# Half of w_up as block products, with down's two accumulators in one bank and part of the quantization on GpSimd

## The reference

```python
w_bot = einsum('bg,got->bot', y, weight * mask);  h = einsum('bnt,bot->bno', x, w_bot) + bias
# _bitlinear(x, w): x quantized per row with 127/max|x|, w quantized to {-1,0,1}/scale
gate = silu(_bitlinear(h, w_gate)); up = _bitlinear(h, w_up)        # 512 -> 2048 each
out  = x + _bitlinear(gate * up, w_down)                            # 2048 -> 512
```

## Time and profile before

| what | value |
|---|---|
| median of the runs | 441.2 us |
| the profiled execution | 440.59 us, span 438.8 us |
| granted TensorE clock | 0.999 |
| PE busy | 425.5 us, 97% of the span |
| DVE busy | 363.5 us, 83% |
| ACT busy | 336.8 us, 77% |
| POOL busy | 205.3 us, 47% |

### The profile page before, as it was taken

The page is one execution under the profiler, slowest core; times in us unless marked ns, Lnnn a source line. Parts: engine busy times, 40 slices in busy tenths (PEclk is TensorE's granted clock), DMA queues, the critical chain, the costliest instruction groups (busy, mean ns, idle before and its releaser), DMA issues.

```text
span 438.8 us, 7668 instructions
## 1 busy us (share of the span) xinstructions
PE 425.5 (97%) x2318; PEld 257.5 (59%) x2318; DVE 363.5 (83%) x611; ACT 336.8 (77%) x474; POOL 205.3 (47%) x221
## 2 busy tenths in 40 slices
PE   4899999999999999999999999999999999999997
PEld 0234688888744455556555565655566555556555
DVE  0327768898897988899999999899999999899992
ACT  1215988778867976888888888888888888888871
POOL 0006999999149995142432423344142333414132
PEclk9999999999999999999999999999999999999999
DMA  7999999995142337254453635535263553535375
GB/s 277 404 396 408 308 335 339 313 251 144 36 98 48 61 66 187 48 145 85 134 120 73 146 70 143 97 118 120 76 157 64 135 115 100 120 87 142 80 162 154
DMA packets 104458, 69.79 MB, mean 159 GB/s; under 512 B 87280, under 2 KB 87536, under 8 KB 102896
## 3 DMA queue, kind: packets, MB, share of 16 engines
q1 hardware_dynamic: 103712, 67.13, 56.9%
q10 hardware_dynamic: 720, 2.36, 1.5%
HBM read 40.11 MB, written 8.39 MB: 111 GB/s over the span
## 4 chain that ended last, share of the span: by engine, by line
PE 59%; DMA 14%; issue 11%; DVE 9%; ACT 5%; POOL 1%; DVEq 0%; ACTq 0%; SPq 0%; POOLq 0%
PE ps L1308 15%; DMA wc<-wc 12%; PE ps L1171 11%; PE ps L1236 10%; PE ps L1126 8%; PE ps L1206 8%; PE ps L1164 4%; ACT wc L640 3%; DVE wc L954 3%; DVE wc L988 2%; DMA wc<-wcond 2%; PE ps L1139 2%; DVE p_part L1006 1%; ACT result L660 1%; PE ps L1243 1%
## 5 line engine op out<-in xcount | busy, mean ns | idle before, releaser
L1171 PE MATMUL ps<-tern_up,qT 128*128 128x512 f16 x512 | 131.1, 379 | 0.0
L1171 PEld LDWEIGHTS ps<-tern_up,qT 128*128 (+1 forms) x512 | 50.0, 98 | 54.5 <-DVE wc L988 0.4
L1006 DVE TENSOR_REDUCE p_part<-wc 128x1 f32<-128x1536 f32 x64 | 77.9, 1217 | 1.7
L988 DVE TENSOR_TENSOR wc<-ps,xT_sb 128x512 f32<-128x512 f32 x104 | 71.1, 683 | 7.3 <-issue 3.3
L640 ACT ACTIVATE wc<-wc 128x1024 f16<-128x1024 f32 x63 | 66.0, 1051 | 4.1 <-DMA wc<-wc 2.1
L623 ACT ACTIVATE wc<-wc,p_scale 128x2048 f32<-128x2048 f32 x30 | 60.1, 2002 | 4.3 <-DVE p_scale L1053 4.3
L1236 PE MATMUL ps<-wc 128*128 128x256 f16 x480 | 62.2, 273 | 0.7 <-DVE wc L954 0.7
L954 DVE TENSOR_TENSOR wc<-wc 128x1024 f16<-128x1024 f16 x60 | 56.9, 949 | 4.5 <-DMA wc<-wc 3.6
L1236 PEld LDWEIGHTS ps<-wc 128*128 128x128 f16 x480 | 46.9, 98 | 18.6 <-issue 1.2
L455 POOL TENSOR_SCALAR out_unit<-p_max,up_step,w_mean 128x1 f32<-128x1 f32 x32 | 11.3, 355 | 99.2 <-DVE p_max L1048 99.2
L618 ACT ACTIVATE xT_sb<-ps,gate_unit 128x512 f32<-128x512 f32 x78 | 49.2, 683 | 10.9 <-PE ps L1206 10.4
(11 more groups left out here) (142 smaller groups left out, 778.3 us busy)
## 6 DMA issues: line engine op xcount, KB each, us to landing
xT_sb<-xT SPq DMA_DIRECT2D x32, 256.0 KB, 6.6
x_res<-x SPq DMA_DIRECT2D x30, 256.0 KB, 2.9
out<-result SPq DMA_DIRECT2D x29, 256.0 KB, 2.4
wc<-wcond SPq DMA_DIRECT2D x12, 512.0 KB, 13.4
wc<-w_gate SPq DMA_DIRECT2D x4, 1024.0 KB, 16.0
wc<-w_up SPq DMA_DIRECT2D x4, 1024.0 KB, 8.4
wc<-w_down SPq DMA_DIRECT2D x4, 1024.0 KB, 6.1
wc<-wcond ACTq DMA_DIRECT2D x4, 512.0 KB, 7.7
```

The costliest lines, as they stand in the source:

```text
L988: nc.vector.tensor_tensor(prod[:, par, 512 * i:512 * i + 512], ps[:, UP + i % 2], source, ALU.mult).then_inc(prod_ready, 1)
L1006: nc.vector.tensor_reduce(p_part[:, par, i:i + 1], prod[:, par, 512 * lo:512 * hi], AX.X, ALU.max, apply_absolute_value=True).then_inc(par ...
L1171: ins = nc.tensor.matmul(ps[:, UP + i % 2], tile_of(s, k), tern_up[:, i, k], start=(k == 0), stop=(k == KH - 1))
```

## The change

**Half of up as block products.** From the pair (10, 11) on, chunks 0 and 2 of `up` become a third group (q = 2) of block products next to the two of gate: 11 pairs, tiles 10 to 31. Chunks 1 and 3 stay plain (`half_chunk`) and share one bank, 1; the group takes banks 0 and 3. Four weight sums are made once on POOL, in steps 6 and 7 (`combine_up`, eight instructions). Per pair ACT gets `copy_ushared` and `copy_useed`, DVE `sum_useed` and `sum_uc22`; the latter leaves its result in `bias_sb` in SBUF, which the product of chunk 2 of the odd tile then reads in place of PSUM.

**Down in one bank.** Bank 3 being taken, down's two accumulators are from pair j = 3 on the halves of bank 2 (the last pair again apart). Where PE would write one half while another engine touches the other, waits are added: `down_product` 1 waits for `copy_shared`, 6 for `scale_c12`, `scale_c11` for product 3, and `scale_c12` for `sum_c22`.

**Moved to POOL.** For even tiles from 8 on POOL rounds (`round_even`, 128x2048) and converts (`convert_even`, two of 128x1024) in ACT's stead, and makes two of the four sums for down (`third_sum`, `second_sum`, 128x1024 f16) in DVE's stead. For tile 30 POOL rounds one half and converts both, ACT rounds the other.

**DVE's order.** The even step takes the largest over chunks 0 and 1, later 2 and 3; the odd step over all four at once. The hardware loop now covers tiles 12 to 27, four turns. SP's code is unchanged.

```diff
-A, B, GA, GB, LAST = 2, 3, (4, 6), (5, 7), (6, 7, UP)
+GA, GB, LAST = (4, 6, 0), (5, 7, 3), (6, 7, UP)
+DOWN, UDOWN = 2, 3
+USTEP = 10
+            def third_sum(j):
+                pool.wait_ge(sum_ready, 2 * j + 2)
+                pool.wait_ge(down_psum, 7 * j - 2)
+                nc.gpsimd.tensor_tensor(qsum[:, 3], q2T[:, b0, KB:KI], qsum[:, 1], ALU.subtract).then_inc(sum3_ready, 1)
+            def round_even(t):
+                pool.wait_ge(p_col, 3 * t + 3)
+                nc.gpsimd.tensor_scalar(prod[:, 0], prod[:, 0], p_scale[:, 0:1], ROUND, ALU.mult, ALU.add).then_inc(even_rounded, 1)
...
+            for t in range(USTEP - 1, TILES - 1, 2):
+                round_even(t - 1)
+                scale_c22((t - 5) // 2)
+                convert_even(t - 1)
+                add_tiles((t - GSTEP + 1) // 2, 3)
+                add_tiles((t - GSTEP + 1) // 2, 2)
+                third_sum((t - 3) // 2)
+                finish_second((t - 5) // 2)
+                unit_of(t)
+                second_sum((t - 3) // 2)
...
+                finish_first((t - 3) // 2)
+                unit_of(t + 1)
...
             def scale_c12(j):
-                act.wait_ge(down_psum, 7 * j + 5)
+                if apart(j):
+                    act.wait_ge(down_psum, 7 * j + 5)
+                else:
+                    act.wait_ge(c22_done, j + 1)
...
+            def sum_uc22(n):
+                dve.wait_ge(group_psum[2], 7 * n + 5)
+                nc.vector.tensor_tensor(bias_sb[:, :], ps[:, GA[2]], ushared, ALU.add).then_inc(gc22_done[2], 1)
...
+            def half_chunk(s, i):
+                final = isinstance(s, int) and s == TILES - 1 and i == 3
+                pe.wait_ge(prod_ready, 4 * s - 1 if final else 4 * s + i - 1)
```

More of the change, by code:

```diff
@@ L502, in _ @@
+            for t in range(USTEP - 1):
                 if t % 2 == 0:
-                    if GSTEP - 2 <= t < TILES - 2:
+                    if GSTEP - 2 <= t:
                         add_tiles((t - GSTEP + 2) // 2, 0)
@@ L804, in _ @@
             scale_down(3)
-            for s in range(0, TILES, 2):
+            for s in range(0, USTEP, 2):
                 even_step(s)
-                odd_step(s + 1)
+                if s + 1 < USTEP - 1:
+                    odd_step(s + 1)
+            for s in range(USTEP - 1, TILES - 2, 2):
+                odd_half_step(s)
+                even_half_step(s + 1)
+            last_step()
             scale_c11(PAIRS - 1)
@@ L1026, in step @@
                     add_blocks(j, 1, b0, b1)
-                    if not last:
+                    if not (isinstance(s, int) and s == USTEP - 1):
                         add_blocks(j, 3, b0, b1)
@@ L1044, in step, with half_step, find_scale @@
                 largest(s, par, 1, 3, 4)
+                find_scale(s, par)
+            def half_step(s, par, j, b0, g, n):
+                last = isinstance(s, int) and s == TILES - 1
+                product(s, par, 0, g, n)
+                if par == 0:
+                    for q in range(2):
+                        sum_gseed(g, q)
+                    sum_useed(n)
+                elif last:
+                    add_blocks(j, 0, b0, b0 + 1)
+                product(s, par, 1, g, n)
+                if par == 1 and not last:
+                    add_blocks(j, 0, b0, b0 + 1)
+                if last:
+                    product(s, par, 2, g, n)
+                if par == 1:
+                    add_blocks(j, 1, b0, b0 + 1)
+                else:
+                    sum_seed(j)
+                    for q in range(2):
+                        sum_gc22(g, q)
+                    largest(s, par, 0, 0, 2)
+                    sum_uc22(n)
+                if not last:
+                    product(s, par, 2, g, n)
+                if last:
+                    largest(s, par, 0, 0, 3)
+                product(s, par, 3, g, n)
+                if par == 0:
+                    sum_c22(j)
+                    largest(s, par, 1, 2, 4)
+                elif last:
+                    largest(s, par, 1, 3, 4)
+                else:
+                    largest_of_all(s, par)
+                find_scale(s, par, last or par == 0)
+            def find_scale(s, par, two=True):
                 if not (isinstance(s, int) and s < 2):
@@ L1215, in down_product @@
                     pe.wait_ge(combo_ready, {0: 1, 3: 3, 6: 4}[i])
-                if i == 1:
+                if i == 0 and not first:
+                    pe.wait_ge(c12_out, j)
+                if i == 0 and isinstance(j, int) and j == PAIRS - 1:
+                    pe.wait_ge(gsilu_ready[0], 4 * GROUPS - 2)
+                if i == 1 and not apart(j):
                     pe.wait_ge(shared_copied, j + 1)
@@ L1219, in down_product @@
                     pe.wait_ge(seed_copied, j + 1)
+                if i == 6 and not apart(j):
+                    pe.wait_ge(c12_out, j + 1)
                 if i == 4:
@@ L1235, in down_product @@
                                     (q2T[:, b1, KB + k], combo[:, 3, k]))[i]
-                    ins = nc.tensor.matmul(ps[:, bank, 0:NB], tile, weight, start=(i < 2 and k == 0), stop=(k == KB - 1),
-                                           skip_group_check=(i >= 2))
+                    ins = nc.tensor.matmul(ps[:, bank, cut], tile, weight, start=(i < (2 if apart(j) else 1) and k == 0), stop=(k == KB - 1),
+                                           skip_group_check=(i >= (2 if apart(j) else 1)))
                 ins.then_inc(down_psum, 1)
@@ L1398, in step @@
                         if i >= 1 and g is not None:
-                            for q in range(2):
+                            for q in range(3 if isinstance(s, int) and s == USTEP - 1 else 2):
                                 group_product(g + 1, q, i - 1, s + 1, 1 - gb)
```

315 lines of the change are left out of this document (243 added, 72 removed).

## The result

The changed kernel takes 443.82 us (median of 6 runs, 443.1 to 445.86) against 440.99 of the kernel before; the ratio is 1.0071, 95% interval 1.0048 to 1.0095. It is slower, by 2.8 us; 4.1 were forecast. The profiled execution has a span of 441.3 us, 2.5 more than before. Three executions ran in a slower state and are left out of the ratios: two of the kernel before (1600.62 and 455.54 us) and one of e4_both (452.92).

A forecast was written before the change was run, and what follows sets the result against it. PE was taken to bound the kernel at 19.07 us per pair, DVE close behind and setting the pace afterwards. Pairs +0.3, turns +1.7, first pair +0.7, tail +1.4 gave +4.1: 445.3 us, range 443 to 448.

The forecast's parts named there:

- the ten pairs: Steady part after the first pair: ten pairs of 19.1 us against 19.07, +0.3 us, with turns counted separately.
- the first pair: PE's extra 1.3 us in step 9 meet a DVE lagging by about half of that: +0.7 us (bounds 0 and 1.3).
- the tail: Step 31: POOL holds DVE, last scale 9.1 us behind tile 30's in place of 7.5: +1.4 us (bounds 0 and 1.6).
- What bounds the kernel: Steady part before the change: PE streams without a gap, 19.07 us per pair, DVE close behind at 18.7.
- The odd step: DVE's step on an odd tile: 7.05 us if not held by POOL, 9.15 with the holds.
- holds: Odd step: POOL's SBUF accesses delay DVE's two sums and the product out of `bias_sb`, 2.1 us together.
- The even step: DVE's step on an even tile: two sums come in, one goes out, from 9.44 to 9.94 us.
- Who sets the pace: Steady pairs after the change: DVE at 19.1 us per pair, against 18.63 of PE.
- Turns: Hardware loop: 0.43 us extra per turn no longer hidden in DVE's slack, four turns +1.7 us (bounds 0 and 1.7).
- PE keeping the pace: Rival for the steady pairs: DVE held under 1.2 us per pair, pairs take 18.63, -2.3 us, 438.9; chance 0.22.
- The loop through POOL and SP: Rival: POOL's work, SP's store, transposes and ACT's convert form a loop of 19.0 to 19.6 us, +7.4, 448.6; chance 0.18.

The follow-up runs named there:

- e4_both: Experiment 4: changed kernel, POOL waits for DVE's chunk 2 product before small scale and converts, `finish_second` directly behind converts; ratio 1.0028 to the kernel before, 441.77 us.
- e5_late: Experiment 5: changed kernel, POOL does small scale and a block sum, waits for DVE's product, then rounds, converts, `finish_second`; ratio 0.9945 to the kernel before, 437.94 us.
- e6_tiny: Experiment 6: changed kernel, POOL rounds and converts only 64 columns each for even tiles 8 to 28, work left out; ratio 0.9940 to the kernel before.
- e2_short: Experiment 2: changed kernel, POOL rounds only 64 of 2048 columns for even tiles 8 to 28, work left out; ratio 1.0026 to the kernel before, 441.29 us.
- e1_order: Changed kernel with `finish_second` directly behind `convert_even` on POOL, ahead of two block sums and `third_sum`; ratio 1.0039 to the kernel before, 441.79 us.
- e3_wait: Changed kernel where POOL, after rounding, waits for DVE's chunk 2 product of the next odd tile before small scale and converts; ratio 1.022 to the kernel before, 450.08 us.
- a0_same: The changed kernel run once more, word for word, as a yardstick; ratio 1.0084 to the kernel before.
- e7_turns: Changed kernel with its hardware loop over tiles 20 to 27 only, two turns in place of four; ratio 1.0157 to the kernel before, 447.39 us.

## Why the prediction was right, and where its terms were off

In short, the mechanism was right, if not whole, and the sizes of its terms were off: the ten pairs were put 2.1 us too high, the first pair and the tail together 1.6 too low. That their sum lies so near the measured time is partly luck.

**What bounds the kernel.** Right. The pairs stayed where they were although PE had less to do: PE was the bound before and no longer is. With GpSimd out of the way (experiments 5 and 6) the pairs take exactly the 18.63 worked out for 86 matmuls at 0.217 us.

**The odd step.** 7.05 free were forecast, 7.10 are measured in e5_late; 2.1 of holds, 1.8 are measured (8.91-7.10). Second sum and product are held where the forecast put it; the first sum's hold is shared with a wait for its transposes. **The even step.** 9.94 forecast, 10.03 measured (9.89 in e2_short); the 0.1 is not resolved.

**Who sets the pace.** The forecast named VectorE alone. That is half of it: three loops lie within 0.3 us of each other. VectorE's own is 18.80 where nothing else interferes (e2_short, no turn); the one through down product 0, `scale_c12`, `finish_first` and the rounding is 18.95 (e4_both); the one through the transposes is as long, within 0.2: among tiles 12 to 30 of the changed kernel ACT's `scale_c12` starts without a wait behind its convert in eight of ten pairs and waits some 0.2 for `sum_c22` in two. e1_order takes this loop away without effect, e3_wait makes it the bound at 19.6 to 19.9. The second was missing from the rivals. It changes no verdict, but it bounds experiment 4 (both edits) at 18.95. Experiment 2 brings little since the converts hold VectorE in the rounding's place.

**Turns.** 0.43 each was forecast, for four turns; three pairs show one, of 0.30 to 0.34 (10.34 and 10.37 against 10.03), and the entry into the loop adds 0.1. That another loop hides the rest is likely and not shown. **The ten pairs** together were put at +2.0 and are -0.06: 18.95 and 19.25 by turns, 19.06 on average over the ten, where I had 19.1 and 0.43. This is the term that was too large: 0.15 too much in each of ten pairs is 1.5, and the turns make the rest.

**The first pair.** +0.7 forecast, +1.07 measured:

```profile
207.53 0.15 DVE L1257 TENSOR_SCALAR p_scale<-p_inv 128x1 f32<-128x1 f32 x1
...
208.34 1.95 DVE L1091 TENSOR_TENSOR wc<-wc 128x1024 f16<-128x1024 f16 x1
...
210.82 1.37 DVE L1091 TENSOR_TENSOR wc<-wc 128x1024 f16<-128x1024 f16 x1
...
220.80 0.43 DVE L1098 TENSOR_TENSOR ps<-ps,w_bot 128x256 f32<-128x256 f32 x1 [0.73 <-ACT result L758]
...
227.56 0.15 DVE L1257 TENSOR_SCALAR p_scale<-p_inv 128x1 f32<-128x1 f32 x1
```

The first sum takes 1.95 and the second 1.37, where 0.68 is free, and in step 10 VectorE waits 0.73 for ACT at 220.80: PE, with its six matmuls more, is late, as the forecast said. The holds do not set this pair's length: it is 20.03 or 20.04 in every variant, also in e5_late and e6_tiny, where the sums take 1.0 and less. The mechanism is the forecast's, and only the share of PE's 1.3 us that comes through was put too low.

**The tail.** +1.4 forecast, +2.6 measured. VectorE's scales and sums, and PE behind them:

```profile
418.15 0.15 DVE L1257 TENSOR_SCALAR p_scale<-p_inv 128x1 f32<-128x1 f32 x1
...
421.18 0.69 DVE L1091 TENSOR_TENSOR wc<-wc 128x1024 f16<-128x1024 f16 x1 [1.94 <-DMA wc<-wc]
...
428.35 0.15 DVE L1257 TENSOR_SCALAR p_scale<-p_inv 128x1 f32<-128x1 f32 x1
```

```profile
422.02 1.03 PE L1473 MATMUL ps<-wc 128*128 128x256 f16 x8 [2.11 <-DVE wc L1091]
...
427.87 3.63 PE L1480 MATMUL ps<-tern_down,wc 128*128 128x512 f16 x16 [1.57 <-DMA wc<-wc]
```

The forecast put the last scale 9.1 behind that of tile 30, by holds alone; it comes 10.20 behind. The first sum waits 1.94 for the transposes of tile 29, PE waits 2.11 for that sum, and again 1.57 for the transposes of tile 30. The transposes of an odd tile are late since the even tile's are, and those wait on SyncE behind `finish_second`. I had this loop as a rival for the pace and did not carry it to the tail, where nothing follows that could cover it. With `finish_second` ahead (e1_order) the last scale is at 8.06: 2.1 of the 2.6 us come back. Behind the last scale nothing changes: from there to the end of the span are 12.9 to 13.0 us in nine of the twelve traces, the kernel before and the changed one among them.

**The rivals.** PE keeping the pace (438.9) is what e5_late does at 437.9, so its price was right (2.3 below the kernel before by forecast, 2.4 measured), and its condition, holds under 1.2 per pair, too: it has none. The loop through POOL and SP, priced at 19.6 per pair if it decides, came true only in e3_wait, with 19.6 to 19.9; in the changed kernel it ties with the others and decides nothing alone.

## What to carry to other kernels

Work moved to an engine with idle time is not free if that engine holds another one at their common memory: ask not only how much it runs but when, beside which instructions. Here one wait and a new order, with every instruction kept, turned a loss of 2.8 us into a gain of 2.4. When two or three loops have nearly the same length, taking one cost away shows nothing; take away several at once (e6_tiny) before a theory is dropped, and ask of every loop in the steady part what it does to the tail.

## What was not expected of the hardware

In the profile of e1_order PE waits 2.38 us before its 16 matmuls of w_down in the tail, and these take 5.14 us in place of 3.63:

```profile
427.18 5.14 PE L1480 MATMUL ps<-tern_down,wc 128*128 128x512 f16 x16 [2.38 <-DMA wc<-wc]
```

The granted clock (third from the end in these rows, ahead of DMA share and GB/s) was 1.00 when the wait began, then 0.50, the lower of the two levels (1.2 GHz), and 1.00 again further on:

```profile
424.00:425.00 1.00, 0.80 (x8) 0.47 (x5) 1.00 (x2) 0.43 (x1) 1.00 (x2) 1.00 2.38 130
428.00:429.00 1.00, 1.00 (x4) 0.44 (x3) 1.00 (x2) 1.00 (x2) 0.00 (x0) 0.50 0.90 219
431.00:432.00 1.00, 1.00 (x7) 0.45 (x5) 0.00 (x0) 0.00 (x0) 0.00 (x0) 1.00 0.97 183
```

The profiled execution of the changed kernel waited 2.11 and 1.57 us in its tail, with four groups of matmuls between, and kept 3.63 for the same 16. But the same kernel once more (a0_same) did lose its clock behind the first of these waits, and 8 matmuls took 1.86 us for the 1.03 of before:

```profile
422.00 1.86 PE L1473 MATMUL ps<-wc 128*128 128x256 f16 x8 [2.10 <-DVE wc L1091]
422.00:423.00 1.00, 1.00 (x5) 0.69 (x6) 1.00 (x2) 0.00 (x0) 1.00 (x2) 0.50 0.13 47
```

There it cost nothing: the 16 matmuls behind had no wait left, and the last scale and the end of the span came when they do in the other execution. In e1_order nothing followed that could cover it, and 14.6 us lie behind the last scale in place of 12.95.

The Trainium skill ("TensorE: Matmul & The Clock Gate", What's actually happening) describes a gate that halves the clock of a PE that has been idle. The traces agree in that all three falls, of e1_order, a0_same and e7_turns, lie in or right behind a wait of PE. They also show that a wait of one length, 2.1 us in one and the same kernel, brings the fall in one execution and not in another, so the length of the wait alone does not foretell it. A late transpose can thus cost more than the wait that it makes: here 1.5 us more.
